# How the stages of a decoder kernel are parted: one barrier or two, and who clears the semaphores

## The reference

```python
def _layernorm(x, axis=-1, eps=1e-05):
    m = jnp.mean(x, axis=axis, keepdims=True)
    v = jnp.var(x, axis=axis, keepdims=True)
    return (x - m) / jnp.sqrt(v + eps)
...
    x = x + _L0_attn_ref(_layernorm(x, axis=-1), L0_attn_Wq, L0_attn_Wk, L0_attn_Wv, L0_attn_Wo)
    x = x + _L0_xattn_ref(_layernorm(x, axis=-1), ctx_1024, ...)
    x = x + _L0_ffn_ref(_layernorm(x, axis=-1), ...)
...
    x = x + _L3_xattn_ref(_layernorm(x, axis=-1), ctx_1024, ctx_1024, L3_xattn_Wq, L3_xattn_Wk, L3_xattn_Wv, L3_xattn_Wo)
    x = x + _L3_ffn_ref(_layernorm(x, axis=-1), L3_ffn_w1, L3_ffn_b1, L3_ffn_w2, L3_ffn_b2)
    return x
```

## Time and profile before

| what | value |
|---|---|
| median of 3 runs | 1182.33 us (1182.02 to 1182.77) |
| the profiled execution's own time | 1173.58 us |
| its span, first to last instruction | 1171.8 us |
| mean granted TensorE clock | 0.837 of 2.4 GHz |
| busy shares of the span | PE 78%, DVE 65%, ACT 49%, POOL 22% |

### The profile page before, as it was taken

How to read it: one execution, slowest core, us unless ns; L and a number is a source line. 1 busy time by engine, 2 the same in 40 slices (tenths; PEclk the granted TensorE clock), 3 DMA queues, 4 the chain that set the end, 5 groups by cost and what they waited for, 6 DMA issues and landing times. The chain is left out here.

```text
span 1171.8 us, 18505 instructions
## 1 busy us (share of the span) xinstructions
PE 919.5 (78%) x6163; PEld 569.5 (49%) x6163; DVE 756.2 (65%) x2181; ACT 571.3 (49%) x1660; POOL 255.0 (22%) x349
## 2 busy tenths in 40 slices
PE   4985499999878356179865889794686999999986
PEld 2345499999746222134543358564582233333323
DVE  6457667777658299354477635632547888888823
ACT  3236367777541311132353434462252677777773
POOL 4006245555400022122202000033400111111100
PEclk8697699999979677566966679797695899999997
DMA  9500000000000620100001000543022011111000
GB/s 228 151 1 1 0 2 2 1 2 2 1 1 1 83 30 0 28 1 1 1 1 51 0 1 1 146 128 96 12 46 63 1 26 25 26 26 21 1 2 14
DMA packets 76176, 35.83 MB, mean 31 GB/s; under 512 B 35226, under 2 KB 74561, under 8 KB 76082
## 3 DMA queue, kind: packets, MB, share of 16 engines
q1 hardware_dynamic: 73714, 33.61, 12.8%
q0 software_dynamic: 896, 0.63, 0.2%
q10 hardware_dynamic: 1472, 0.41, 0.2%
HBM read 24.42 MB, written 11.05 MB: 30 GB/s over the span
## 5 line engine op out<-in xcount | busy, mean ns | idle before, releaser
L519 ACT ACTIVATE L3x_E<-L3x_pS 128x400 f32<-128x400 f32 (+1 forms) x384 | 167.8, 507 | 48.6 <-PE L3x_pS L613 47.6
L435 DVE TENSOR_REDUCE L3x_NMP<-L3x_pM 128x1 f32<-128x361 f32 x384 | 178.1, 524 | 18.7 <-PE L3x_pM L591 17.8
L591 PE MATMUL L3x_pM<-ctx_tm 64*128 64x361 bf16 x384 | 104.4, 341 | 14.0 <-DVE L3x_NMP L435 9.0
L613 PE MATMUL L3x_pS<-ctx_tm 64*128 64x400 bf16 (+1 forms) x384 | 107.6, 350 | 3.4 <-ACT L3x_E L519 2.1
L1465 ACT ACTIVATE L0x_E<-L0x_E,ctx_r 128x100 f32<-128x100 f32 x288 | 105.1, 369 | 9.3 <-DVE L0x_E L1372 9.3
L628 PE MATMUL L3x_pO<-L3x_E,CT 128*32 128x400 f32 (+1 forms) x768 | 85.2, 516 | 0.0
L591 PEld LDWEIGHTS L3x_pM<-ctx_tm 64*128 64x128 bf16 x384 | 30.4, 96 | 110.2 <-DVE L3x_NMP L435 90.8
L1554 PE MATMUL L0x_pU<-ctx_tm,L0x_E 128*100 128x129 f32 x576 | 70.5, 279 | 3.1 <-POOL L0x_E L1285 3.1
L1544 PE MATMUL L0x_pS<-L0x_QS,CT 128*128 128x100 f32 x576 | 70.4, 280 | 0.0
L1554 PEld LDWEIGHTS L0x_pU<-ctx_tm,L0x_E 128*100 128x100 f32 x576 | 67.2, 171 | 4.6 <-POOL L0x_E L1285 4.1
L1285 POOL TENSOR_TENSOR L0x_E<-L0x_E,L0x_RZ 128x1200 f32<-128x1200 f32 x24 | 52.6, 2193 | 75.0 <-DVE L0x_RZ L1392 75.0
(11 more groups left out here) (631 smaller groups left out, 2132.6 us busy)
## 6 DMA issues: line engine op xcount, KB each, us to landing
ctx_tm<-in_ctx SPq DMA_DIRECT2D x8, 704.0 KB
ctx_tm<-key_terms SPq DMA_DIRECT2D x16, 270.8 KB, 4.2
key_terms<-ctx_tm SPq DMA_DIRECT2D x42, 90.2 KB
ctx_tm<-in_L_ffn_wi SPq DMA_DIRECT2D x4, 512.0 KB, 7.6
ctx_tm<-in_L_ffn_wo SPq DMA_DIRECT2D x4, 512.0 KB, 7.7
ctx_tm<-query_terms SPq DMA_DIRECT2D x16, 75.0 KB, 3.4
slots_in<-L2a_zeros SPq DMA_DIRECT2D x8, 129.0 KB
L2f_XS<-slots_in SPq DMA_DIRECT2D x4, 258.0 KB, 3.0
```

The source lines that it names most:

```text
L435: nc.vector.tensor_reduce(NMP[:, p, i // NC4, a, i % NC4:i % NC4 + 1], v, AX.X, ALU.max, negate=True).then_inc(s_mr, 1)
L519: nc.scalar.activation(E[0:r, n % EB, :], pS[0:r, n % 3, 0:NG * T], ACT.Exp, scale=SCALE8).then_inc(s_e, 1)
L591: nc.tensor.matmul(pM[:, n % 3, 0:CW], key_rows(QS, a)[:, b, p, 128 * x:128 * x + 128], key_rows(KS, a)[:, b % KB, c, p, :], start=True, s ...
L613: nc.tensor.matmul(pS[0:NW[k], n % 3, 0:NG * T], key_rows(KS, a)[:, b % KB, k % 4, p, 128 * (k // 4):128 * (k // 4) + NW[k]], key_rows(QS, ...
```

## The change

Stages take their semaphores from two halves of 48 in turn (160 to 207 and 208 to 255). When a stage ends, its half is cleared by a plain instruction of GpSimd, with no barrier around it; the next stage works with the other half meanwhile, and the half is used again only a stage later, behind another Block's barrier in which GpSimd takes part. All 15 Blocks drop `no_gpsimd_drain=True`: their barrier is then of the second kind, one round in which the drains do the counting and GpSimd is drained as well.

```diff
 class Stage:
...
-    FIRST_SEM = 160
+    FIRST_SEM, HALF_SEMS = 160, 48
+    count = 0
 
     def __init__(self, nc, ctx, name):
-        self.nc, self.ctx, self.name, self.next = nc, ctx, name, self.FIRST_SEM
+        self.nc, self.ctx, self.name = nc, ctx, name
+        self.first = self.FIRST_SEM + self.HALF_SEMS * (Stage.count % 2)
+        Stage.count += 1
+        self.next = self.first
         ctx.callback(self.clear)
 
     def clear(self):
 
-        self.nc.all_engine_barrier(sems_to_clear=range(self.FIRST_SEM, self.next))
+        self.nc.gpsimd.sem_clear(range(self.first, self.next))
...
     def sem(self, name):
+        if self.next == self.first + self.HALF_SEMS:
+            raise ValueError(f"{self.name} has more semaphores than half of the stages' range")
         self.next += 1
...
-        with nc.Block(no_gpsimd_drain=True) as block:
+        with nc.Block() as block:
```

## The result

| | before | after |
|---|---|---|
| median of the first comparison | 1181.08 us (6 executions, 1173.53 to 1182.77) | 1165.65 us (6 executions, 1162.44 to 1170.62) |
| ratio | | 0.9893, 95% interval 0.9859 to 0.9927 |
| span of the profiled execution | 1171.8 us | 1166.3 us |
| its mean granted clock | 0.837 | 0.850 |

The forecast was 1172.1 us, a ratio of 0.9913 to the 1182.33 us it started from, with a range of 1168.5 to 1176.0. Of the 6.4 us between forecast and measurement, 1.2 us is the median of the kernel before, which fell from 1182.33 to 1181.08 us when three executions more were added; the other 5.2 us is a gain of 15.4 us between the medians where 10.2 was forecast. The two profiled spans differ by 5.5 us only, half of what was forecast, and the medians by 15.4 us.

A forecast was written before the change was run, and what follows sets the result against it. Barriers at stage ends, uncovered by other work, were taken to lie on the path. Savings of 8.6 + 0.6 + 0.45 + 0.5 + 0.05 = 10.2 us from 1182.33 gave 1172.1 us, range 1168.5 to 1176.0.

The forecast's parts named there:

- A stage end lies on the path, one round is 0.32 us.: At stage ends nothing covers the barrier; with one round left at 0.32 us, VectorE's 11 gaps save 8.6 us.
- L3f's end: Where SyncE goes on alone: two rounds of 0.75 us plus a clear, less 0.32, saves 0.5 us.
- The first stage's end: Only the second round with its clear (0.4 us) and an EVENT_SEMAPHORE (0.05) go: 0.45 us saved; wait for x stays.
- GpSimd's long drain goes from the path: At L2f's end the 2.0 us drain, issued in the Block, has 9.6 us of cover; gap falls 2.92 to 0.32.
- The clear is covered: After each release GpSimd clears alone, 51 to 283 ns, within its idle time; nothing of it is exposed.
- rival 3: At Block ends the drain takes 2.0 us at 14 more ends with GpSimd last: 1200 us, slower; chance 0.03.
- rival 4: At stage starts something else holds the first instruction; gaps stay near 0.8 us, 1181 to 1182 us; chance 0.03.
- rival 2: At L2f's end the drain stays on the path, 2.0 us come back: 1174.1 us; chance 0.05.
- I take the gain as it is and put it on their median: Whole kernel: 10.2 us taken from the runs' median of 1182.33 us, 8.75 us above the profiled execution's sum.
- +-2.5 us around the forecast: Whole kernel: allowance for PE's clock changing at other moments within the stages, shifts expected mostly to cancel over 14.
- Rival 1: PE's clock changes shift within stages: 1176 to 1178 us if later (chance 0.05), 1167 if earlier (0.04).
- the stages' own lengths change by more than the gaps do: Sign of a wrong forecast, over the stages between barriers; they were expected as long as before to some 0.5 us.

The follow-up runs named there:

- the footing of eight extra matmuls: Eight overwritten transposes added in nine stages, to the changed kernel and the kernel before: 1156.63 us (0.9856) and 1173.16 us (1.0013).
- the longer clear: Changed kernel with the clear made four times at each stage end, over a whole half of 48 semaphores: 1161.39 us, ratio to before 0.9912.
- the lone clear: Changed kernel with the old Blocks (`no_gpsimd_drain=True`), so GpSimd is drained nowhere; halves and clear without barrier stay: ratio to before 0.9906.

## Why the prediction was right in its steps and missed the time

- *A stage end lies on the path, one round is 0.32 us.* Right. The gaps after are 0.30 to 0.31 us. The 11 gaps saved 8.7 us (8.6 forecast), L0a's end 0.64 (0.6).
- *L3f's end.* Right: 0.54 us where 0.5 was forecast. The 0.05 us at `store_block`'s end is too small beside the store's landing to be read.
- *The first stage's end.* 1.67 to 1.00 us, 0.67 where 0.45 was forecast. This gap holds the landing of x, and it moved by itself: 1.67 and, in the row below, 1.20 us in the two profiles of the kernel before. The share of the barrier in it was not measured apart.

```profile
6.05 1.06 DVE L83 BATCH_NORM_STATS2 stats<-X 100x6 f32<-100x128 f32 x5 [1.20 <-PEq L58]
```

- *GpSimd's long drain goes from the path.* Right, shown from both sides: 2.92 to 0.30 us with it covered, 2.60 with the cover taken away, 0.95 with only its place changed.
- *The clear is covered.* Right: four times as many, over more semaphores, cost nothing.
- *The drain is dear (rival 3), the gap is not the barrier (rival 4), the drain stays (rival 2).* All fell.
- *The step that failed is the last one: "I take the gain as it is and put it on their median", together with "+-2.5 us around the forecast" for the clock.* The median of 1182.33 us was itself at the upper edge of what the kernel before gives. Its profiled execution at 1173.58 us was the more usual one. The forecast saw the 8.75 us between the two, said that no row told why, and then left them out of the range. The term of +-2.5 us had no row behind its size. In the later comparisons the kernel before had medians of 1170.8 to 1173.5 us. Starting from 1172.4 us, the same 10.2 us give 1162.2, and the changed kernel measured 1162.49 beside it. In the first comparison itself the base was off by 1.2 us only; there it was the gain of 15.4 us between two medians of six, which the range had no room for. Single executions of one program scatter over 8 to 9 us within a comparison (changed kernel 1158.6 to 1167.4), not 5.
- *Rival 1, the clock moves.* It was there, and underrated. No run shows the clock in GHz. Where the record says 1.2 and 2.4 GHz, the runs show granted clocks of 0.50 and 1.00, with 12 and 24 matmuls in about the same busy time (2.44 and 2.46 us). The estimate "over 14 stages such shifts should mostly cancel" is not borne out: one L2a alone differs by 2.9 us between two executions of the same program, the stages together were 5.1 us longer after the change in the first pair of profiles, and on the footing of eight extra matmuls they were some 7 us shorter. The forecast also gave as a sign of being wrong that the stages' own lengths change by more than the gaps do. In sum they did not in the first pair (5.1 against 10.4 us), but L1a, L1x, L2a, L2x and L2f each changed by more than its own gap, by up to 4.4 us.
- *What was luck.* The ratio of 0.9913 lies within the intervals of both comparisons. The barriers' 10.4 us are shown. That the stages' shifts left the ratio there was not foreseen: on the footing of eight extra matmuls the same change is worth 0.0157.

What stays open: why the first three executions of the kernel before took 1182 us, since neither a profile nor the granted clock of such an execution is on record; whether the changed kernel's own gain holds 0 or some 2 us from the clock beyond its barriers (the ratios 0.9893, 0.9903 and, with the longer clear, 0.9912 stand for 12.5, 11.4 and 10.3 us of 1172, and 10.4 us would be 0.9911); why L1a was longer in both profiles of the changed kernel, and L2f in its first; and what, in the change, moves the clock's rises and falls within the stages.

## What to carry to other kernels

Where a barrier holds all engines, as here, the whole idle stretch is on the path, so read it as a gap (0.4 us between the two releases of ctxn's end), not from the durations of the instructions in it (0.12 us), and multiply by the number of barriers. Let the engine with a slow drain reach it early, behind one barrier instead of two (L2f's gap fell from 2.92 to 0.30 us), and let bookkeeping such as clearing semaphores run behind the release on an engine that has time (56 clears of 285 ns left the ratio at 0.9912, beside 0.9903). Before you put a forecast gain on a median, compare the median with the profiled execution and with other executions of the same program: where they differ by as much as the gain, forecast the ratio, and let the range hold that difference. In a kernel of many short stages a mean clock over a stage can stay the same while the low stretch moves onto its matmuls (L2f had 0.80 in the kernel before and in the second profile of the changed one, with 38 matmuls at 1.00 and 16 at 0.52 in the same 7 us stretch), so compare the same stretch of work, with its number of matmuls.

## What the runs showed of the hardware that was not expected

- One more whole barrier with nothing to wait for costs 0.33 us at most places in the program (three add 0.98 us at L0x's end). At some places one engine's next instruction comes 0.3 to 0.45 us late, with no wait in the profile: 0.68 us instead of 0.38 at L0a's end with the lone clear, 1.26 to 1.44 us instead of 0.98 for three rounds at five ends. The two profiles of the kernel before agree in their gaps to 0.01 us behind the first, but each of these variants was profiled once, so whether such a delay stays with its place in the program is not shown.
- The first drain of GpSimd after its indirect DMAs took 2022 ns in two different programs, some 10 us after the last of them, and 34 ns at the median of the ends of the kernel before. Issued early, in the changed kernel, it ended 2.2 us behind the last of them.
- Clearing 48 semaphores takes 285 ns, 3 take 51: some 5 ns each.
- With eight short extra matmuls in each of nine stages TensorE was busy for less time in L2x than without them (58.3 us against 60.8 in the changed kernel and 62.9 in the one before), at a granted clock of 0.97 against 0.92 and 0.89.
- The same 10 us at the start of L1x, with PE busy for 9.3 us in each, held 40 matmuls at a granted clock of 0.66 in both profiles of the kernel before and 28 at 0.51 and 0.52 in those of the changed one.
